# ScalarE's order in a batch of attention: contexts later, one copy of values taken over, one exponential moved up

## The chip, the cores and the metric

The kernel runs on one core of a Trainium2 chip. The metric is device time in microseconds (us) of one execution, all loads from HBM and the stores included. Three runs of the kernel before took 789.79, 789.86 and 788.10 us; their median is 789.79.

## The reference

Two layers work on x of 16 sequences with 128 tokens and 128 features (float32). The change touches only the attention at the head of the first one. For each of the 16 sequences (here: batches):

```python
qkv = (x @ Wqkv.T + bqkv)                       # 16 heads of width 8
attn = softmax(q @ k.T / sqrt(8))               # per head, 128 x 128
coh = sigmoid(tanh([x, cond] @ Wc1.T + bc1) @ Wc2.T + bc2)
mod = attn * coh;  mod = mod / (mod.sum(-1) + 1e-8)
mod = (1 - 0.21) * mod + 0.21 * fa              # fa: one row of weights per batch
x1 = (mod @ v) @ Wout.T + bout
```

After the attention come a product-key expert layer with a batch normalisation over all tokens, a mixture of 8 experts, and a second mixture with hidden width 512. They are unchanged.

## The kernel before

The kernel is written without a scheduler: each engine has its own list of instructions in a fixed order, and semaphores are waited for and raised by hand. An engine that waits holds up everything behind it in its list. Each engine's list for the attention has a function `attend(b, ...)` that is called once per batch b. The stages overlap: while the probabilities of batch b are transposed, the scores of b + 1 are computed and the inputs of b + 2 are projected.

One batch, in the order of the data, with the line that the profile gives:

- PE `project(b)` multiplies the batch's x with four weights into PSUM bank 7 (L461): queries, keys, values, context.
- ScalarE `queries_keys(b)` copies queries (L919) and keys (L921) out of bank 7. ScalarE `values_context(b)` copies the values to v_stage (L925) and takes the tanh of the context (L927); PE's next `project` waits for that tanh (semaphore s_tanh), and so does `coherence(b)`.
- POOL `head_keys(b)` spreads the keys by head, one instruction of 128x512 (L358), when the keys are copied and the scores of b - 1 are through. POOL also stages x (L352) and adds the bias to the values (`values`, L343).
- PE `scores(b)` (L461, 32 rows by 512 columns) waits for L358 and for DVE's last subtraction of the batch before, and fills banks 2 to 5.
- DVE `row_max` (L1205) and `minus_max` (L1212), for the halves q = 0 and 1; ScalarE `exps(b, q)` (L931), an exponential of 128x1024 in place.
- PE `transposes(b, q)` (L501), eight transposes into banks 0 and 1; ScalarE `probs_T(b, q)` (L936) copies both banks to SBUF. Both halves use the same two banks, so the second half's transposes wait for the first half's L936.
- PE `values(b, q)` (L461, 32 small matmuls in all) puts heads' outputs into bank 0 (q = 0) and bank 1 (q = 1). DVE `keep_values(b, q)` (L1219) copies each to oT_heads, and PE `gather(b, q)` brings them to token-major form.
- ScalarE's `ec` (L960) is an exponential of 16 columns from DVE's `tl` (L1281); DVE's cden (L1298), zden (L1302), reciprocal (L1304), o_n (L1306) and o_s (L1312) finish the attention output.
- One batch later: PE `out_T` (L529) transposes it, ScalarE `out_T` (L942) copies it, PE `out_proj` multiplies it with Wout, in the middle of the second half's transposes, and ScalarE `out_x1` (L949) adds the bias.

PE's order in `attend(b)` is: transposes(b, 0), scores(b + 1), out_T(b - 1), transposes(b, 1) with out_proj(b - 1) between its halves, project(b + 2), values(b, 0), values(b, 1), a sum of values, coherence(b + 1), gather(b, 0), gather(b, 1). DVE's order is: tl, row_max(b + 1, 0), minus_max(b + 1, 0), row_max(b + 1, 1), both keep_values(b), minus_max(b + 1, 1), then cden to o_s. In batch 2 DVE also scales the layer's keys (L1252, twice, and L1255), behind minus_max.

ScalarE's order in `attend(b)` before the change is: probs_T(b, 0), out_T(b - 1), out_x1(b - 1), probs_T(b, 1), ec, queries_keys(b + 2), exps(b + 1, 0), exps(b + 1, 1), values_context(b + 2).

Of the kernel before, what the change touches and what calls it, by code (L numbers as in the profile page):

```python
# [22 lines left out]
ACT = mybir.ActivationFunctionType  # L23
# [59 lines left out]
def program(nc, xtok, xT, pA, pL, pC, pR, p8, wq, wqT, down, up, w1, w2, w3, f1, f2, out):  # L83
# [7 lines left out]
    with ExitStack() as ctx:  # L91
# [3 lines left out]
        def sem(name):  # L95
            return ctx.enter_context(nc.semaphore(name))
# [36 lines left out]
        oT_heads = junk[:, 0:512]  # L133
# [23 lines left out]
        def A(name, a=0, b=None):  # L157
            lo, hi = A_AT[name]
            return apack[:, lo + a:hi if b is None else lo + b]
# [5 lines left out]
        def R(name, rows_=P):  # L165
            lo, hi = R_AT[name]
            return rows[0:rows_, lo:hi]
# [54 lines left out]
        def bank(n, a=0, b=512):  # L222
            return banks[:, n, a:b]
# [15 lines left out]

        s_S, s_mx, s_D, s_E, s_T, s_ET, s_pv = (sem("att_" + n) for n in ("S", "mx", "D", "E", "T", "ET", "pv"))  # L240

        s_O, s_sel = sem("att_O"), sem("att_sel")
        s_zd, s_rz, s_on, s_os, s_ostore = sem("s_zd"), sem("s_rzatt"), sem("s_on"), sem("s_os"), sem("s_ostore")

        s_oTp, s_oT, s_x1p, s_x1 = sem("s_oTp"), sem("s_oT"), sem("s_x1p"), sem("s_x1")
# [29 lines left out]
        def wait(eng, s, value):  # L275

            if not isinstance(value, int) or value > 0:
                eng.wait_ge(s, value)

        def col(ap, i):  # L280
            return ap[:, ds(i, 1)] if not isinstance(i, int) else ap[:, i:i + 1]

        def cols(ap, i, n=P):
            return ap[:, ds(i * n, n)] if not isinstance(i, int) else ap[:, i * n:(i + 1) * n]
# [174 lines left out]
        def _(pe):  # L459
            def mm(o, l, r, start=True, stop=True):  # L460
                return pe.matmul(o, l, r, start=start, stop=stop)  # L461
# [33 lines left out]
            def transposes(b, q):  # L495

                pe.wait_ge(s_E, 2 * b + q + 1)
                wait(pe, s_ET, 2 * b + q)
                wait(pe, s_O, 2 * b)
                for g in range(8):  # L500
                    m = pe.transpose(bank(g // FG, P * (g % FG), P * (g % FG) + P), D[q][:, P * g:P * g + P], A("ident"))  # L501
                    if g == 3 and q == 1 and b > 0:
                        out_proj(b - 1)
                m.then_inc(s_T, 1)
# [11 lines left out]

            def gather(b, q):

                pe.wait_ge(s_O, 2 * b + q + 1)
                for j in range(2 * q, 2 * q + 2):  # L520
                    m = mm(bank(6, 9 * FG * j, 9 * FG * j + WIDE), oT_heads[:, P * j:P * j + P], A("sel"))
                if q == 1:
                    m.then_inc(s_sel, 1)
# [7 lines left out]
            def out_proj(b):  # L531
                pe.wait_ge(s_oT, b + 1)
                mm(bank(6, 240, 368), A("woT"), oT).then_inc(s_x1p, 1)
# [377 lines left out]
        def _(act):  # L911
# [3 lines left out]
            def queries_keys(b):  # L915

                act.wait_ge(s_proj, b + 1)
                wait(act, s_S, FG * b)
                act.activation(qT, bank(7, 0, P), ACT.Identity, bias=A("bq"))  # L919
                wait(act, s_kh, b)  # L920
                act.activation(kT, bank(7, P, 2 * P), ACT.Identity, bias=A("bk")).then_inc(s_q, 1)  # L921

            def values_context(b):
                wait(act, s_v, b)
                act.activation(v_stage, bank(7, 2 * P, 3 * P), ACT.Copy).then_inc(s_vst, 1)  # L925
                wait(act, s_coh, b)
                act.activation(thT, bank(7, 3 * P, 4 * P), ACT.Tanh, bias=col(hidb, b)).then_inc(s_tanh, 1)  # L927

            def exps(b, q):
                act.wait_ge(s_D, 2 * b + q + 1)  # L930
                act.activation(D[q], D[q], ACT.Exp, scale=float(HD) ** -0.5).then_inc(s_E, 1)  # L931

            def probs_T(b, q):
                act.wait_ge(s_T, 2 * b + q + 1)
                wait(act, s_pv, 2 * (b - 1) + q + 1)
                act.activation(ET[q], banks[:, 0:2, :].rearrange("p c n -> p (c n)"), ACT.Copy).then_inc(s_ET, 1)  # L936

            def out_T(b):
                act.wait_ge(s_oTp, b + 1)
                wait(act, s_x1p, b)  # L940
                if b < SEEN:
                    m = act.activation(oT, bank(6, 240, 368), ACT.Copy, accum_out=col(o_sum, b))  # L942
                else:
                    m = act.activation(oT, bank(6, 240, 368), ACT.Copy)
                m.then_inc(s_oT, 1)

            def out_x1(b):
                act.wait_ge(s_x1p, b + 1)
                act.activation(cols(x1T_all, b), bank(6, 240, 368), ACT.Identity, bias=A("bout"),  # L949
                               accum_out=col(x1_sum, b)).then_inc(s_x1, 1)  # L950

            def attend(b, more, project_more, first=False):
                probs_T(b, 0)
                if not first:
                    out_T(b - 1)
                    out_x1(b - 1)
                probs_T(b, 1)
                act.wait_ge(s_tl, b + 1)
                wait(act, s_cden, b)
                act.activation(ec, tl, ACT.Exp, scale=-1.0).then_inc(s_ec, 1)  # L960
                if project_more:
                    queries_keys(b + 2)
                if more:
                    exps(b + 1, 0)
                    exps(b + 1, 1)
                if project_more:
                    values_context(b + 2)

            act.wait_ge(dve_setup, DVE_SETUP.index("hid_bias") + 1)
            act.wait_ge(pe_setup, PE_SETUP.index("field2") + 1)  # L970
# [5 lines left out]
                           accum_out=small[0:B, 11:12]).then_inc(act_setup, 1)  # L976
            exps(0, 0)
            exps(0, 1)
            values_context(1)
            attend(0, True, True, first=True)  # L980
            for b in range(1, B - 2):
                attend(b, True, True)
# [183 lines left out]
        def _(v):  # L1166
# [36 lines left out]
            def row_max(b, q):  # L1203
                v.wait_ge(s_S, FG * b + FG)
                v.tensor_reduce(mx4[:, 8 * q:8 * q + 8],  # L1205
                                groups(banks[:, 2 + 2 * q:4 + 2 * q, :].rearrange("p c n -> p (c n)")),
                                AX_X, ALU.max).then_inc(s_mx, 1)
# [5 lines left out]
                                mx4[:, 8 * q:8 * q + 8].unsqueeze(2).broadcast_to([P, 8, P]),  # L1213
                                ALU.subtract).then_inc(s_D, 1)

            def keep_values(b, q):

                v.wait_ge(s_pv, 2 * b + q + 1)
                v.tensor_copy(oT_heads[:, 256 * q:256 * q + 256], bank(q, 0, 256)).then_inc(s_O, 1)  # L1219

            def shifted_scores(b):
                row_max(b, 0)
                minus_max(b, 0)
                row_max(b, 1)
                keep_values(b - 1, 0)
                keep_values(b - 1, 1)
                minus_max(b, 1)

            row_max(0, 0)
# [48 lines left out]
            def attend(b, more):  # L1278
                v.wait_ge(s_coh, b + 1)
                wait(v, s_ec, b)  # L1280
                v.tensor_tensor(tl, bank(6, 368, 368 + NH), R("bc2"), ALU.add).then_inc(s_tl, 1)  # L1281
                if b == B - 2:
                    shift()
                if b == B - 1:
                    centre_last(B - 2)
                    centre(3)
                    keep_values(b, 0)
                    keep_values(b, 1)
                if more:
                    shifted_scores(b + 1)  # L1290
                if b == 2:
                    scaled_keys_of_weights()
                if b == B - 2:
                    for c in range(3):
                        centre(c)

                v.wait_ge(s_ec, b + 1)
                v.tensor_scalar(cden, ec, 1e-8 / (1 - FIELD), (1 + 1e-8) / (1 - FIELD), ALU.mult, ALU.add).then_inc(s_cden, 1)  # L1298
                v.wait_ge(s_sel, b + 1)
                v.wait_ge(s_cden, b + 1)  # L1300
                o9 = bank(6, 0, 144).rearrange("p (h d) -> p h d", d=9)
                v.tensor_tensor(zden.unsqueeze(2), o9[:, :, HD:HD + 1], cden.unsqueeze(2), ALU.mult).then_inc(s_zd, 1)  # L1302
                v.wait_ge(s_zd, b + 1)
                v.reciprocal(rz_att, zden).then_inc(s_rz, 1)  # L1304
                v.wait_ge(s_rz, b + 1)
                v.tensor_tensor(o_n.rearrange("p (h d) -> p h d", d=HD), o9[:, :, 0:HD],  # L1306
                                rz_att.unsqueeze(2).broadcast_to([P, NH, HD]), ALU.mult).then_inc(s_on, 1)
                v.wait_ge(s_on, b + 1)
                v.wait_ge(s_vs, b + 1)
                wait(v, s_oTp, b)  # L1310
                wait(v, s_ostore, min(b, B - 2))
                v.scalar_tensor_tensor(o_s, bank(6, 384, 512), col(fas, b), o_n, ALU.mult, ALU.add).then_inc(s_os, 1)  # L1312
# [432 lines left out]
```

## Time and profile before

| | |
|---|---|
| median of three runs | 789.79 us |
| profiled execution | 790.0 us |
| its span, first to last instruction | 788.2 us |
| PE busy | 740.4 us (94%) |
| DVE busy | 563.2 us (71%) |
| ACT (ScalarE) busy | 569.2 us (72%) |
| POOL busy | 314.9 us (40%) |
| mean granted TensorE clock | 0.989 of full speed |

The first and the last instruction of the profiled execution are 788.2 us apart, and 1.8 us lie around them. The attention takes about the first 150 us of the span. In the rows below, starts are us from the beginning of the span. An instruction that does not depend on the one before it on its engine can start before that one's recorded end. L461, L501 and L529 are PE's; region is one large SBUF tensor in which most tensors of the attention lie, so its name says little; G_both takes the transposed probabilities and W_both the probabilities.

### The profile page before, as it was taken

What the parts mean: (1) busy time and instruction counts of PE and PEld (TensorE: products, weight loads), DVE (VectorE), ACT (ScalarE), POOL (GpSimd) and SP (SyncE); (2) the same over time, 40 slices, a digit from 0 to 9 for tenths busy, and PEclk for the clock granted to TensorE, in tenths of its full rate; (3) what the DMA queues carried; (4) which work ended last, traced back from release to release, by engine and by line L of the source; (5) the groups of instructions that cost most, each with busy time, mean ns of one, the idle gap of its engine ahead of it and who ended that gap; (6) DMA issues with size and microseconds to landing.
All of it is one profiled execution on the core that took longest, in us unless ns stands there. A gap on an engine that the chain in (4) does not pass through costs nothing.

```text
span 788.2 us, 14848 instructions
## 1 busy us (share of the span) xinstructions
PE 740.4 (94%) x5314; PEld 653.7 (83%) x5314; DVE 563.2 (71%) x1511; ACT 569.2 (72%) x985; POOL 314.9 (40%) x230
## 2 busy tenths in 40 slices
PE   4989898979887999999999999999999999999998
PEld 3767676859775799899989989999898899999887
DVE  3788889579379877976986797688679756833422
ACT  2577777359797878978988896898789788553243
POOL 2122231079987175344727442563646071000000
PEclk9999999999997999999999999999999999999999
DMA  8930000000000000000000000000000000000000
GB/s 311 343 108 1 2 2 1 2 1 2 1 1 0 1 1 7 2 1 1 7 2 1 9 0 2 1 8 1 1 2 7 1 1 8 1 1 8 1 1 7
DMA packets 11016, 16.92 MB, mean 21 GB/s; under 512 B 664, under 2 KB 6976, under 8 KB 10688
## 3 DMA queue, kind: packets, MB, share of 16 engines
q1 hardware_dynamic: 10944, 15.98, 6.3%
q8 instruction: 43, 0.70, 0.4%
q14 instruction: 29, 0.24, 0.1%
HBM read 14.93 MB, written 1.05 MB: 20 GB/s over the span
## 4 chain that ended last, share of the span: by engine, by line
PE 84%; DVE 7%; issue 4%; ACT 4%; DMA 1%; SPq 0%; POOL 0%; DVEq 0%; ACTq 0%; POOLq 0%
PE banks L461 78%; PE banks L501 3%; ACT G_both L936 2%; PE banks L698 2%; DVE W_both L1418 1%; DMA region<-in_pR 1%; DVE W_both L1212 1%; ACT region L1006 1%; DVE acc L1563 1%; PE banks L529 1%; DVE HF L1424 0%; ACT region L1012 0%; PE banks L730 0%; DVE pairs L1382 0%; ACT x1T_all L949 0%
## 5 line engine op out<-in xcount | busy, mean ns | idle before, releaser
L403 POOL TENSOR_TENSOR region<-sim 128x1024 f32<-128x1024 f32 x128 | 260.8, 2065 | 99.7 <-DVE top_keys L1375 63.2
L1068 ACT ACTIVATE HF<-banks,lpack 128x256 f32<-128x256 f32 x256 | 105.4, 479 | 55.6 <-PE banks L461 54.6
L1006 ACT ACTIVATE region<-region,neg_thr 128x1024 f32<-128x1024 f32 x128 | 143.8, 1153 | 0.0
L1418 DVE SCALAR_TENSOR_TENSOR W_both<-region,rz_rel,W_both 128x1024 f32<-128x1024 f32 x98 | 137.7, 1405 | 1.7
L461 PE MATMUL banks<-HF,w_sb 128*128 128x256 f32 x512 | 125.0, 388 | 7.8 <-DVE HF L1424 7.7
L461 PEld LDWEIGHTS banks<-f_sb,HF 128*128 128x128 f32 x1024 | 123.7, 192 | 3.4
L1012 ACT ACTIVATE region<-region,dtop 128x1024 f32<-128x1024 f32 x114 | 125.3, 1142 | 0.0
L461 PE MATMUL banks<-f_sb,HF 128*128 128x128 f32 x1024 | 124.5, 275 | 0.0
L461 PE MATMUL banks<-cT,f_sb 128*128 128x256 f32 x512 | 122.7, 382 | 0.1
L461 PEld LDWEIGHTS banks<-HF,w_sb 128*128 128x128 f32 x512 | 95.6, 194 | 20.2 <-DVE HF L1424 8.7
L461 PEld LDWEIGHTS banks<-cT,f_sb 128*128 128x128 f32 x512 | 92.1, 190 | 16.3 <-issue 2.9
L461 PE MATMUL banks<-region 128*128 128x128 f32 (+6 forms) x606 | 90.5, 378 | 8.9 <-DMA region<-in_pC 5.7
L1058 ACT ACTIVATE H<-banks,lpack 128x256 f32<-128x256 f32 x128 | 53.3, 468 | 49.6 <-PE banks L461 49.6
L461 PEld LDWEIGHTS banks<-region 128*128 128x128 f32 (+1 forms) x606 | 67.1, 200 | 19.3 <-issue 11.2
L411 POOL COPY x_all<-x2s 128x128 f32<-128x128 f32 x16 | 11.5, 722 | 163.7 <-DVE x2s L1434 163.7
L1424 DVE TENSOR_SCALAR HF<-banks,lpack 128x256 f32<-128x256 f32 x128 | 55.8, 477 | 23.9 <-PE banks L461 23.6
L461 PEld LDWEIGHTS banks<-w_sb,H 128*128 128x128 f32 x512 | 65.9, 192 | 6.7 <-ACT H L1058 2.8
L461 PE MATMUL banks<-w_sb,H 128*128 128x128 f32 x512 | 68.5, 277 | 2.1 <-DVE acc L1563 1.0
L1563 DVE SCALAR_TENSOR_TENSOR acc_f<-banks,cw,acc_f 128x128 f32<-128x128 f32 x112 | 34.0, 345 | 50.9 <-PE banks L461 50.1
L461 PE MATMUL banks<-x2T,w_sb 128*128 128x256 f32 x256 | 67.1, 385 | 0.0
L461 PEld LDWEIGHTS banks<-x2T,w_sb 128*128 128x128 f32 x256 | 47.6, 193 | 6.3 <-issue 0.5
L931 ACT ACTIVATE W_both<-W_both 128x1024 f32<-128x1024 f32 x32 | 33.9, 1059 | 21.3 <-DVE W_both L1212 21.3
(164 smaller groups left out, 976.1 us busy)
## 6 DMA issues: line engine op xcount, KB each, us to landing
w_sb<-in_w SPq DMA_DIRECT2D x1, 2048.0 KB, 13.0
f_sb<-in_f SPq DMA_DIRECT2D x1, 2048.0 KB, 16.0
region<-in_wq SPq DMA_DIRECT2D x1, 1024.0 KB, 9.0
region<-in_wqT SPq DMA_DIRECT2D x1, 1024.0 KB, 10.8
w_sb<-in_w SPq DMA_DIRECT2D x1, 1024.0 KB, 8.6
out_x<-acc_f SPq DMA_DIRECT2D x16, 64.0 KB, 1.6
region<-in_pA SPq DMA_DIRECT2D x1, 848.5 KB, 4.7
x1T_all<-in_xT SPq DMA_DIRECT2D x1, 768.0 KB, 8.0
```

The source lines that it names most:

```text
L403: pool.tensor_tensor(S[a][h].rearrange("p (i j) -> p i j", i=NK), sim[a][:, h, :].unsqueeze(2).broadcast_to([P, NK, NK]), sim[a][:, PH + h ...
L461: return pe.matmul(o, l, r, start=start, stop=stop)
L501: m = pe.transpose(bank(g // FG, P * (g % FG), P * (g % FG) + P), D[q][:, P * g:P * g + P], A("ident"))
L698: m = pe.transpose(bank(c // 4, P * (c % 4), P * (c % 4) + P), W[a][:, P * c:P * c + P], ident[:, :])
L931: act.activation(D[q], D[q], ACT.Exp, scale=float(HD) ** -0.5).then_inc(s_E, 1)
L1006: act.activation(S[a][h], S[a][h], ACT.Prelu, bias=neg_thr[t % 4][:, h:h + 1], alpha=STEEP).then_inc(h_L, 1)
L1012: act.activation(W[a] if h == 0 and t > 1 else S[a][h], S[a][h], ACT.Exp, bias=dtop[t % 4][:, h, 7:8]).then_inc(h_E, 1)
L1058: m = act.activation(H2[e % 2][:, n, :], bank(H2_BANK[e], 256 * n, 256 * n + 256), ACT.Relu, bias=L("b2", 2 * e + n, 2 * e + n + 1))
L1068: m = act.activation(HF[e % 2][:, f, :], bank(2 + b, 256 * (f % 2), 256 * (f % 2) + 256), ACT.Gelu_apprx_tanh, bias=L("bf", 4 * e + f, 4 * ...
L1418: v.scalar_tensor_tensor(W[a], S[a][h], rz_rel[a][:, h:h + 1], W[a], ALU.mult, ALU.add).then_inc(h_w, 1)
L1424: m = v.tensor_scalar(H1[e % 2][:, n, :], bank(H1_BANK[e], 256 * n, 256 * n + 256), L("b1", 2 * e + n, 2 * e + n + 1), 0.0, ALU.add, ALU.max)
L1563: m = v.scalar_tensor_tensor(dst[:, a, :], y, weight, base, ALU.mult, ALU.add)
```

## The change

ScalarE gets another order for a batch, and one copy goes from DVE to ScalarE:

- probs_T(b, 0), ec, out_T(b - 1), values_context(b + 1), probs_T(b, 1), out_x1(b - 1), keep_values(b) for the first half, exps(b + 1, 0), queries_keys(b + 2), exps(b + 1, 1).
- values_context runs for b + 1 in attend(b), where it ran for b + 2; the call for batch 1 ahead of the loop is gone.
- DVE's keep_values copies the second half alone.
- The semaphore s_O, which counted both copies, becomes s_O0 and s_O1, since two engines now raise them. PE's transposes wait for both and each gather for its own.

```diff
-                wait(pe, s_O, 2 * b)
+                wait(pe, s_O0, b)
+                wait(pe, s_O1, b)
...
-                pe.wait_ge(s_O, 2 * b + q + 1)
+                pe.wait_ge((s_O0, s_O1)[q], b + 1)
...
+            def keep_values(b):
+                act.wait_ge(s_pv, 2 * b + 1)
+                act.activation(oT_heads[:, 0:256], bank(0, 0, 256), ACT.Copy).then_inc(s_O0, 1)
+
             def attend(b, more, project_more, first=False):
                 probs_T(b, 0)
-                if not first:
-                    out_T(b - 1)
-                    out_x1(b - 1)
-                probs_T(b, 1)
                 act.wait_ge(s_tl, b + 1)
                 wait(act, s_cden, b)
                 act.activation(ec, tl, ACT.Exp, scale=-1.0).then_inc(s_ec, 1)
+                if not first:
+                    out_T(b - 1)
+                if more:
+                    values_context(b + 1)
+                probs_T(b, 1)
+                if not first:
+                    out_x1(b - 1)
+                keep_values(b)
+                if more:
+                    exps(b + 1, 0)
                 if project_more:
                     queries_keys(b + 2)
                 if more:
-                    exps(b + 1, 0)
                     exps(b + 1, 1)
-                if project_more:
-                    values_context(b + 2)
...
             exps(0, 0)
             exps(0, 1)
-            values_context(1)
...
-            def keep_values(b, q):
-
-                v.wait_ge(s_pv, 2 * b + q + 1)
-                v.tensor_copy(oT_heads[:, 256 * q:256 * q + 256], bank(q, 0, 256)).then_inc(s_O, 1)
+            def keep_values(b):
+
+                v.wait_ge(s_pv, 2 * b + 2)
+                v.tensor_copy(oT_heads[:, 256:512], bank(1, 0, 256)).then_inc(s_O1, 1)
...
-                keep_values(b - 1, 0)
-                keep_values(b - 1, 1)
+                keep_values(b - 1)
...
-                    keep_values(b, 0)
-                    keep_values(b, 1)
+                    keep_values(b)
```

## Rows read from the trace of the kernel before

**Rows 1.** Busy time by stretch: length, busy us per engine, PE clock, DMA share, GB/s.
```profile
42.31:50.82 8.51, 7.12 (x81) 5.55 (x80) 8.14 (x16) 5.79 (x15) 1.98 (x4) 1.00 0.52 145
50.82:127.98 77.16, 69.81 (x792) 55.34 (x791) 67.83 (x121) 56.75 (x131) 19.79 (x40) 1.00 0.01 2
127.98:135.70 7.72, 6.99 (x81) 5.53 (x79) 7.16 (x15) 5.58 (x13) 1.79 (x3) 1.00 0.00 0
```

**Rows 2.** Chain of waits within one batch: start, length, what.
```profile
94.04 1.07 PE banks L461 x8
...
95.37 0.42 issue
```

**Rows 3.** Timeline of ScalarE in one batch: start, length, engine, line, operation.
```profile
89.40 1.02 ACT L936 ACTIVATE G_both<-banks 128x1024 f32<-128x1024 f32 x1
...
90.43 0.36 ACT L919 ACTIVATE region<-banks,region 128x128 f32<-128x128 f32 x1
90.68 0.37 ACT L921 ACTIVATE region<-banks,region 128x128 f32<-128x128 f32 x1
...
93.30 1.06 ACT L931 ACTIVATE W_both<-W_both 128x1024 f32<-128x1024 f32 x1 [1.31 <-DVE W_both L1212]
94.26 0.26 ACT L925 ACTIVATE region<-banks 128x128 f32<-128x128 f32 x1
...
94.67 1.02 ACT L936 ACTIVATE G_both<-banks 128x1024 f32<-128x1024 f32 x1
```

**Rows 4.** Timeline of DVE in the same batch.
```profile
91.27 0.86 DVE L1219 COPY region<-banks 128x256 f32<-128x256 f32 x2
...
93.18 0.17 DVE L1298 TENSOR_SCALAR region<-region 128x16 f32<-128x16 f32 x1
...
94.54 0.17 DVE L1281 TENSOR_TENSOR region<-banks,region 128x16 f32<-128x16 f32 x1
```

**Rows 5.** Two copies of 128x256 from PSUM by source line (ns min/median/max).
```profile
L1219 DVE COPY region<-banks x32: 424/424/425, 28.7 to 148.0; 128x256 f32<-128x256 f32 x32
...
L1042 ACT ACTIVATE cT<-banks x8: 366/383/386, 268.0 to 754.4; 128x256 f32<-128x256 f32 x8
```

**Rows 6.** Timeline of DVE and PE in the step into batch 3.
```profile
46.09 1.28 DVE L1252 TENSOR_TENSOR region<-region 128x512 f32<-128x512 f32 x2
...
48.78 0.17 DVE L1281 TENSOR_TENSOR region<-banks,region 128x16 f32<-128x16 f32 x1
...
49.10 0.30 PE L529 MATMUL banks<-region 128*128 128x128 f32 x1 [1.08 <-DVE region L1281]
```

**Rows 7.** Timeline of POOL and PE in the batch of rows 3.
```profile
91.12 1.04 POOL L358 TENSOR_TENSOR region<-region 128x512 f32<-128x512 f32 x1 [3.86 <-ACT region L921]
...
93.97 1.14 PE L461 MATMUL banks<-region 32*128 32x512 f32 x8
95.04 0.33 PE L529 MATMUL banks<-region 128*128 128x128 f32 x1
```

**Rows 8.** Timeline of POOL and PE at batch 0.
```profile
10.72 1.04 POOL L358 TENSOR_TENSOR region<-region 128x512 f32<-128x512 f32 x1 [3.61 <-ACT region L921]
...
11.90 1.24 PE L461 MATMUL banks<-region 32*128 32x512 f32 x4 [2.08 <-POOL region L358]
```

**Rows 9.** Timelines of DVE and POOL in the expert stages, where they meet.
```profile
209.63 2.39 POOL L403 TENSOR_TENSOR region<-sim 128x1024 f32<-128x1024 f32 x1
...
211.97 0.21 DVE L1400 TENSOR_TENSOR dtop<-top 128x64 f32<-128x64 f32 x1
211.98 1.96 POOL L403 TENSOR_TENSOR region<-sim 128x1024 f32<-128x1024 f32 x1
...
230.79 1.09 DVE L1488 COPY picked<-best 128x4 f32<-128x4 f32 x1
...
241.68 3.00 DVE L1418 SCALAR_TENSOR_TENSOR W_both<-region,rz_rel,W_both 128x1024 f32<-128x1024 f32 x1
241.69 1.91 POOL L403 TENSOR_TENSOR region<-sim 128x1024 f32<-128x1024 f32 x1
```

More of the change, by code:

```diff
@@ L240, in program @@
         s_S, s_mx, s_D, s_E, s_T, s_ET, s_pv = (sem("att_" + n) for n in ("S", "mx", "D", "E", "T", "ET", "pv"))
-        s_O, s_sel = sem("att_O"), sem("att_sel")
+        s_O0, s_O1, s_sel = sem("att_O0"), sem("att_O1"), sem("att_sel")
         s_zd, s_rz, s_on, s_os, s_ostore = sem("s_zd"), sem("s_rzatt"), sem("s_on"), sem("s_os"), sem("s_ostore")
```

## The prediction

> **What bounds the kernel now.** I read the page first, then busy time by stretches, then the chain of waits in one batch, then the timeline of that batch for each engine. PE's share is near full on the page's busy line, but it is an average over stages, and the change touches the attention stage alone. So the question is what paces that stage. The windows [rows 1] are cut at the starts of ScalarE's second copy of transposed probabilities (L936, probs_T(b,1)); I call such a start E. A batch takes 7.72 us. Thirteen of the steps from E of batch 0 (26.88) to E of batch 14 (135.70) do: the one at 127.98, two like it, and ten in 50.82:127.98 (77.16 us). The step from batch 2 to 3 takes 8.51, since DVE has three extra instructions there (L1252 twice, L1255). The step behind 135.70 is of another form: DVE's centring and the out_T behind it set its end. In a regular batch no engine is full: of 7.72 us PE is busy 6.99, DVE 7.16 and ACT 5.58 in that window.
>
> The chain [rows 2] stays on PE from the values through gather, transposes, scores and out_T, and then stands 0.42 us at 95.37. ScalarE's timeline [rows 3] says why: the next transposes need the banks that L936 empties, and L936 started at 94.67 although the first transposes were over by 94.04, where the chain goes on with the scores. It was behind the value copy and tanh (L925, L927: from 94.26 to 94.67, 0.41 us), and these behind the exponential at 93.30, which waited for DVE. So today's loop is values, two copies on DVE, subtraction, exponential, value copy and tanh, L936, transposes, L936, values.
>
> All places below are us after E = 89.40.
>
> **What the change takes away.** Value copy and tanh leave the stretch between exponential and L936 for the idle time after out_T: 0.41 us a batch off that loop. Their new place has room: out_T's copy starts there at 6.4 and the next E is at 7.8, and ScalarE's old x1 copy in that hole has moved behind E. The first copy of values leaves DVE, but this shortens nothing on the loop: the pair took 0.86 us where one takes 0.424 [rows 4, 5], so the second did not overlap the first and was waiting for its own matmuls. It stays at 91.27 + 0.86 - 0.42 = 91.71, or 2.31. At most it would start 0.09 us earlier (the overlap that 90.43 and 90.68 show between two ScalarE instructions of 0.36), and the exponential that it feeds is not on the new path. By this loop alone the step would be 7.72 - 0.41 = 7.31. PE has a floor of its own: without the 0.42 us stand, out_T would still end at 5.97 (95.37), and from there to E there is a fixed piece. Batch 3 shows that piece bare [rows 6]: out_T ends at 49.10 + 0.30 = 49.40, E follows at 50.82, that is 1.42 us (copy, out_proj, second half of the transposes). 5.97 + 1.42 = 7.39: the most that the change could give is 0.33 us a batch.
>
> **What it puts in the way.** Scores of the next batch but one need the keys' per-head product on POOL (L358), and this needs queries_keys, which now stands behind three things. Step by step:
> - The first copy of values on ScalarE starts when PE has delivered: DVE's started at 91.27, and DVE was waiting, so 1.87. I take the same for ScalarE; it could be 0.02 earlier or later.
> - A 128x256 copy from PSUM takes 0.383 on ScalarE [rows 5]. What follows starts 0.10 before an instruction's end there (93.30 + 1.06 against 94.26, 90.43 + 0.36 against 90.68) [rows 3], so after 0.28: exps(b+1,0) starts at 2.15.
> - Exponential to next instruction: 93.30 to 94.26, 0.96. Queries at 3.11.
> - queries to keys 0.25 (90.43 to 90.68): keys at 3.36. Keys to L358 0.44 (90.68 to 91.12) [rows 7]: L358 at 3.80. It takes 1.04: end 4.84.
> - From its end to PE: batch 0 has it bare [rows 8], 10.72 + 1.04 = 11.76, scores at 11.90, so 0.14. Scores at 4.98.
> Now they start at 93.97, or 4.57 [rows 7], in line behind the transposes. From their start to out_T's end 95.04 + 0.33 - 93.97 = 1.40; then the piece of 1.42. E to E becomes 4.98 + 1.40 + 1.42 = 7.80, against 7.72: plus 0.08 us, 13 times, 1.1 us. The cover that queries_keys loses is thus just larger than the gain: L358 used to end at 2.76, with 1.8 us to spare.
>
> The moved ec (L960, tiny) and x1 do not bind: x1 is wanted by a matmul behind the values, and T0 (first transposes, 3.60) wants the exponential that ends at 2.15 + 1.06 = 3.21. The two semaphores add a wait that is already met. In the step into batch 3 out_T is late for DVE's sake (49.10) and remains so. The last step and the tail are set by DVE's centring and by PE; the table load moves behind the copy of values but is still over before out_T of batch 15. I cost these at nothing; were the cover of the table load gone, it would cost at most 1 us once.
>
> **A collision.** Moving L358 from 1.72 to 3.80 puts it on DVE's cden (L1298, 93.18, or 3.78) [rows 4]. Small DVE instructions can stand still while POOL works: a copy of 4 columns took 1.09 us at 230.79 [rows 9]. The Trainium skill, "SBUF — State Buffer", section "Who interferes with whom", says that tensor_scalar and copy in a two-port mode, and DVE instructions with two SBUF inputs, need a port pair that GpSimd holds for its whole instruction, whoever starts first. This trace agrees with the blocking (the 1.09). By that page alone L358 would have to wait for cden's 0.17, and the step would be 7.97.
> Near ties [rows 9]: the 128x64 subtraction at 211.97 was 0.01 us ahead of POOL; it took 0.21, too short for a wait, and POOL took 1.96. But the weighted sum at 241.68, ahead by as little, took 3.00 beside a POOL instruction of 1.91: it waited that one out. cden is small and 0.02 ahead, so I take the first: L358 is 0.05 to 0.06 longer, the step 7.86, plus 0.14. Bounds: nothing (7.80), and cden held to L358's end. In that case cden ends at about 4.86 instead of 3.95, tl starts 0.91 later than 94.54 (5.14 now), at 6.05; out_T follows tl by 0.32 (48.78 to 49.10) [rows 6], at 6.37, and E by 1.72 (49.10 to 50.82), at 8.09: plus 0.37.
> In batch 2 the two 128x512 products of L1252 (1.28 us together) [rows 6] start where cden else does. The nearest row is a POOL instruction that met such a DVE sum of 128x512 just ahead of it: 2.39 for 1.91, 0.48 [rows 9]. L358 would end at 5.3, the second product would wait for it, from 4.4 to about 5.3, and all behind it to E too: plus 0.9, once. Between 0 and 1.1.
>
> **Sum.** 13 x 0.14 = 1.8 and 0.9: plus 2.7 us. The profiled execution took 790.0 (span 788.2), the median is 789.79; 789.8 + 2.7 = 792.5. All after attention hangs on it in series and on loads that are in by 50 us, so the sum passes through.
>
> **Rivals.**
> 1. *The collision costs nothing*, cden being out of L358's way: 13 x 0.08 = 1.1, 790.9. For it: cden reads 16 columns, and 0.05 us decides. The legs of the sum are good to 0.07 a batch together, so this case reaches from 789.9 to 791.9. Chance 0.30.
> 2. *POOL wins*: L358 takes the port first and cden waits each time: 13 x 0.37 + 0.9 = 5.7, 795.5. For it: the row at 241.68; 0.02 us is less than what I know of the copy's start. Against it: the row at 211.97. Chance 0.20.
> 3. *Faster*: the 0.42 us stand goes and nothing takes its place. It needs scores at 4.57 or earlier, so the key chain shorter by 0.41 than its legs above; then 7.39, 13 x 0.33 = 4.3 less, 785.5. It decides at E to scores: every 0.1 below 4.90 is 1.3 us gained against now. Only a copy on ScalarE that starts well before DVE's could do it, and it can't before PE has finished. Chance 0.08.
> The forecast (792.5, own range 791.2 to 794.0) has 0.40; 0.02 is left.
>
> **How the numbers follow.** No change means within 0.3%, 2.4 us, about what a measurement here can tell. The forecast lies mostly above that line: slower 0.28, same 0.12. Rival 1 is same (0.28) and slower (0.02), rival 2 slower (0.20), rival 3 faster (0.08). With the rest: slower 0.51, same 0.40, faster 0.09. Range 789.9 to 795.9: below it rival 3 and the edge of rival 1, above it little of rival 2.
>
> **What the profile after would show.** L936 to L936 of 7.8 to 7.9 us; the PE stand of 0.42 gone from behind out_T and one of 0.3 to 0.4 between first transposes and scores, released by L358; L358 at 3.8 after E, long 1.04 (rival 1) or 1.1; cden 0.17 long, or about 1.0 (rival 2); out_proj released by ScalarE's out_T copy. In batch 2 L1252 longer than 1.28 for two. I am wrong if scores start right behind the transposes (rival 3), if the copy on ScalarE doesn't start near 1.87, or if L358 is no longer what PE waits for.

## The result, and the profile after

The changed kernel takes 792.3 us (median of 18 runs), the kernel before beside it 789.62 (18 runs): ratio 1.0032, 95% interval 1.0021 to 1.0043, so 2.5 us slower (1.7 to 3.4). The forecast was 792.5. The profiled execution of the changed kernel took 793.8 (span 792.0).

Busy time by stretch, changed kernel, cut at E (columns as in [rows 1], which these rows answer):

```profile
34.62:42.39 7.77, 7.13 (x81) 5.57 (x80) 6.37 (x12) 6.09 (x15) 1.93 (x4) 1.00 1.05 353
42.39:51.77 9.38, 7.19 (x81) 5.59 (x80) 8.88 (x15) 6.19 (x14) 2.97 (x4) 1.00 0.49 134
51.77:129.42 77.65, 71.28 (x792) 55.64 (x791) 63.26 (x111) 60.83 (x141) 19.38 (x40) 1.00 0.01 2
137.09:145.96 8.87, 6.16 (x73) 5.34 (x72) 7.29 (x15) 5.16 (x10) 0.46 (x1) 1.00 0.01 2
145.96:792.00 646.04, 623.56 (x4075) 562.40 (x4073) 448.27 (x1298) 478.42 (x783) 282.18 (x157) 0.98 0.01 3
```

A regular step is 7.76 to 7.77 us (77.65 for ten; the first is 7.81, the last 7.67) where it was 7.72, and the step into batch 3 is 9.38 where it was 8.51. The last step is shorter, 8.87 against 9.60: before's trace has PE at half clock (1.2 GHz) for 3.4 us of it, from 143.3; e3, whose regular steps are those of before, takes 8.87 there at full clock. E of batch 15 comes 0.66 us later than before (145.96 against 145.30); without that half-clock time it would be 1.4. The last row has the rest of the kernel, in which nothing was changed: 646.04 against 642.90.

Timeline of one batch of the changed kernel, all engines, E = 82.83. It answers to [rows 3, 4, 7]; L937 was L936, L932 was L931, L955 is ScalarE's new copy, L920 and L922 are queries and keys, L1303 is cden, L530 is out_T:

```profile
82.83 1.02 ACT L937 ACTIVATE G_both<-banks 128x1024 f32<-128x1024 f32 x1 [0.59 <-PE banks L502]
...
84.70 0.38 ACT L955 ACTIVATE region<-banks 128x256 f32<-128x256 f32 x1 [0.50 <-PE banks L461]
84.98 1.05 ACT L932 ACTIVATE W_both<-W_both 128x1024 f32<-128x1024 f32 x1
...
85.92 0.36 ACT L920 ACTIVATE region<-banks,region 128x128 f32<-128x128 f32 x1
86.17 0.37 ACT L922 ACTIVATE region<-banks,region 128x128 f32<-128x128 f32 x1
...
86.61 0.17 DVE L1303 TENSOR_SCALAR region<-region 128x16 f32<-128x16 f32 x1
86.62 1.05 POOL L358 TENSOR_TENSOR region<-region 128x512 f32<-128x512 f32 x1 [5.83 <-ACT region L922]
86.72 1.06 ACT L932 ACTIVATE W_both<-W_both 128x1024 f32<-128x1024 f32 x1 [0.18 <-DVE W_both L1219]
...
87.69 1.01 ACT L937 ACTIVATE G_both<-banks 128x1024 f32<-128x1024 f32 x1
87.77 1.14 PE L461 MATMUL banks<-region 32*128 32x512 f32 x8 [0.31 <-issue]
...
88.84 0.33 PE L530 MATMUL banks<-region 128*128 128x128 f32 x1
...
90.59 1.02 ACT L937 ACTIVATE G_both<-banks 128x1024 f32<-128x1024 f32 x1 [0.59 <-PE banks L502]
```

Read it as distances from E: copy 1.87, exponential 2.15, queries 3.09, keys 3.34, head product 3.79, scores 4.94, out_T 6.01, next E 7.76. The chain of the changed kernel shows PE's stand where it was forecast, ahead of the scores, and none behind out_T, where [rows 2] had 0.42:

```profile
86.59 0.87 PE banks L502 x8
87.47 0.31 issue
87.77 1.14 PE banks L461 x8
88.91 0.26 PE banks L530
89.17 0.44 PE banks L502 x4
```

The step into batch 3, DVE and POOL (answers to [rows 6]; L1258 are the two key products):

```profile
46.17 2.13 DVE L1258 TENSOR_TENSOR region<-region 128x512 f32<-128x512 f32 x2
46.18 1.57 POOL L358 TENSOR_TENSOR region<-region 128x512 f32<-128x512 f32 x1 [5.83 <-ACT region L922]
...
47.70 0.75 POOL L352 COPY region<-x1T_all 128x128 f32<-128x128 f32 x1
...
50.05 0.30 PE L530 MATMUL banks<-region 128*128 128x128 f32 x1 [1.06 <-DVE region L1287]
```

The two products take 2.13 us instead of 1.28, the head product 1.57 instead of 1.04, and the small copy behind it 0.75 instead of 0.29: each waits for the other side. PE stands 0.82 us ahead of the scores, where before it stood nowhere, and 1.06 ahead of out_T, as before (1.08). It is DVE's delay that sets this step: tl (L1287, at 49.74) comes 7.35 after E where it came 6.47 (48.78), and out_T waits for it; the later scores are through by then.

### The profile page after: what moved, and what is told of

The parts are those of the page before. It is cut to its first block, busy times and chain, and to the rows that moved or that the text cites. A ratio compares the mean times of both kernels' runs of the same rounds, so it can differ in the third digit from the quotient of the medians.

```text
span 792.0 us, 14878 instructions
## 1 busy us (share of the span) xinstructions
PE 745.3 (94%) x5314; PEld 656.4 (83%) x5314; DVE 556.9 (70%) x1495; ACT 575.6 (73%) x1001; POOL 315.3 (40%) x230
## 3 DMA queue, kind: packets, MB, share of 16 engines
HBM read 14.93 MB, written 1.05 MB: 20 GB/s over the span
## 4 chain that ended last, share of the span: by engine, by line
PE 87%; DVE 5%; ACT 4%; issue 3%; DMA 1%; POOL 0%; DVEq 0%; SPq 0%; ACTq 0%; POOLq 0%
PE banks L461 80%; PE banks L502 4%; ACT G_both L937 2%; PE banks L699 2%; DVE W_both L1423 1%; ACT region L1019 1%; DVE W_both L1219 1%; ACT region L1013 1%; DMA region<-in_pC 1%; PE banks L530 1%; DVE acc L1568 0%; PE banks L731 0%; DVE pairs L1387 0%; DVE PT L1520 0%; PE banks L790 0%
## 5 line engine op out<-in xcount | busy, mean ns | idle before, releaser
L461 PE MATMUL banks<-x2T,w_sb 128*128 128x256 f32 x256 | 69.0, 394 | 0.0
L358 POOL TENSOR_TENSOR region<-region 128x512 f32<-128x512 f32 x16 | 17.3, 1082 | 95.8 <-ACT region L922 95.8
```

What stands on the lines that cost most here:

```text
L358: pool.tensor_tensor(k_heads.rearrange("p (g n) -> p g n", g=FG), kT.unsqueeze(1).broadcast_to([P, FG, P]), A("head4").unsqueeze(2).broadc ...
```

## Experiments

My theory: the change frees 0.4 us a batch behind the exponential and loses it, and more, to the chain queries_keys, head product, scores; the copy on ScalarE gains nothing; key scaling and head product collide once. Rivals: the copy on ScalarE is what costs, or DVE's share is what binds, or the rest of the kernel pays. Ratios are against runs of the kernel before on the same chip (788.6 us in the first group, 789.3 in the second, 788.9 in the third).

**e1: keys ahead of the copy.**

```diff
+                if project_more:
+                    queries_keys(b + 2)
                 keep_values(b)
                 if more:
                     exps(b + 1, 0)
-                if project_more:
-                    queries_keys(b + 2)
-                if more:
                     exps(b + 1, 1)
```

> The changed kernel, with queries_keys ahead of ScalarE's copy of the first values and of exps(b+1,0). Places are us after E, the start of ScalarE's second L936-type copy of a batch. Theory (the key chain queries_keys, POOL's head product, scores paces the changed kernel): the head product starts at about 2.0 instead of 3.8, scores start right behind the first transposes at 4.57, and a step from E to E takes 7.39 to 7.43 us instead of 7.76 in the changed kernel and 7.72 before. The collision with DVE's key scaling in batch 2 goes too: that step takes 8.5, not 9.38. Sum against before: 13 x -0.31 = -4.0 us, about 785.5 us. Rival (the copy on ScalarE is what costs): the step stays at 7.7 or more and the time is not below that of before.

784.18 us, ratio 0.9948 (0.9935 to 0.9960): 4 us faster than before. In its timeline (here of the one step that takes 7.54) the head product starts 1.97 after E and scores 4.57:

```profile
93.61 1.02 ACT L937 ACTIVATE G_both<-banks 128x1024 f32<-128x1024 f32 x1 [0.59 <-PE banks L502]
...
95.58 1.04 POOL L358 TENSOR_TENSOR region<-region 128x512 f32<-128x512 f32 x1 [3.78 <-ACT region L922]
...
98.18 1.14 PE L461 MATMUL banks<-region 32*128 32x512 f32 x8
```

Twelve steps are 7.30 to 7.43 us, one is 7.54 (in it out_T came late, at 99.43), and the step into batch 3 is 8.50. With one call moved, the change's loss of 2.5 us is a gain of 4: the key chain is the cause. (This takes in the step into batch 3, 0.88 of it.)

**e2: contexts later, all copies of values left on DVE, keys first.** The kernel before, with `attend` in this order. ec and out_x1 stand in their new places too, and the call for batch 1 ahead of the loop is gone:

```diff
                 probs_T(b, 0)
-                if not first:
-                    out_T(b - 1)
-                    out_x1(b - 1)
-                probs_T(b, 1)
...
                 act.activation(ec, tl, ACT.Exp, scale=-1.0).then_inc(s_ec, 1)
+                if not first:
+                    out_T(b - 1)
+                if more:
+                    values_context(b + 1)
+                probs_T(b, 1)
+                if not first:
+                    out_x1(b - 1)
...
-                if project_more:
-                    values_context(b + 2)
```

> The kernel before, with only the contexts a batch later (and x1 behind the second transposed copy, ec early); queries_keys ahead of the exponentials; DVE keeps both copies of values. Theory: the whole gain comes from this part. DVE's second row maximum now ends at about 2.1 after E, so its two copies of values start some 0.1 to 0.2 later than with one on ScalarE; step 7.43 to 7.50, key scaling step 8.5, sum -2.9 to -3.8 us, about 786 to 787 us. Rival (moving a copy off DVE is what a shorter step needs): step stays near 7.7, no change from before.

785.66 us, ratio 0.9956 (0.9944 to 0.9969), regular step 7.39 (7.43 to 7.50 expected). DVE's two copies did start late (96.03, 2.00 after E) but took 0.74 together instead of 0.86, so its subtraction started at 2.66 as ever (96.69; before 92.05, 2.65):

```profile
96.03 0.74 DVE L1219 COPY region<-banks 128x256 f32<-128x256 f32 x2
96.69 1.21 DVE L1212 TENSOR_TENSOR W_both<-banks,region 128x1024 f32<-128x1024 f32 x1
...
97.93 1.06 ACT L931 ACTIVATE W_both<-W_both 128x1024 f32<-128x1024 f32 x1 [1.07 <-DVE W_both L1212]
98.90 1.01 ACT L936 ACTIVATE G_both<-banks 128x1024 f32<-128x1024 f32 x1
```

So the gain needs no copy on ScalarE, and it is the contexts': L936 follows the exponential by 0.97 us (97.93 to 98.90) where it was 1.37 (93.30 to 94.67), and PE's stand of 0.42 is gone from the chain. ec and out_x1, moved with them, show no part in it. out_x1 had stood ahead of E, but E follows the end of the transposes by 0.04 before and by 0.03 in e2, and the exponential waits for DVE's subtraction in both.

**e3: the copy on ScalarE, nothing else.** The kernel before, with DVE's, PE's and the semaphores' part of the change, and on ScalarE:

```diff
                 if project_more:
                     queries_keys(b + 2)
+                keep_values(b)
                 if more:
                     exps(b + 1, 0)
```

> The kernel before, with only the first copy of values on ScalarE, between queries_keys and exps(b+1,0); contexts stay at the end. Theory: DVE's second copy already waited for its own matmuls, so the loop through DVE's subtraction, exponential, contexts and transposed copies is as long as before: step 7.72, sum 0 (within 0.5 us). Rival (DVE's share is the bound): each batch 0.34 shorter, -4.4 us. Rival (the copy on ScalarE costs): longer steps.

788.97 us, ratio 1.0006 (0.9997 to 1.0015); regular step 7.71 to 7.72. Neither DVE's share nor the copy's cost on ScalarE sets the step.

**e4: the changed kernel, contexts back at the end.**

```diff
                 if not first:
                     out_T(b - 1)
-                if more:
-                    values_context(b + 1)
                 probs_T(b, 1)
...
                 if more:
                     exps(b + 1, 1)
+                if project_more:
+                    values_context(b + 2)
```

> The changed kernel with values_context back at the end of a batch, so only the move of the contexts is undone. Theory: with the key chain binding, the contexts' new place is worth nothing: step 7.76 to 7.80, key scaling step 9.4, the time within 0.5 us of the changed kernel's 792.3, about 2.5 us above before. Rival (the contexts' move does gain 0.41 in the changed kernel and something else costs more): step about 8.1 to 8.2, about 797 us.

797.85 us, ratio 1.0110 (1.0094 to 1.0125), step 8.41. My expectation (7.76 to 7.80, about 792) was wrong by 6 us. The rival's time, about 797, was met, but its step of 8.1 to 8.2 was not. The timeline names what I had left out:

```profile
93.29 0.45 POOL L343 TENSOR_TENSOR region<-region 128x128 f32<-128x128 f32 x1
...
93.77 0.28 ACT L926 ACTIVATE region<-banks 128x128 f32<-128x128 f32 x1 [0.57 <-POOL region L343]
93.95 0.36 ACT L928 ACTIVATE region<-banks,region 128x128 f32<-128x128 f32 x1
94.20 1.03 ACT L937 ACTIVATE G_both<-banks 128x1024 f32<-128x1024 f32 x1
```

The value copy overwrites v_stage, so it waits for POOL's `values`, and in POOL's list this stands behind the head product and the staging of x. With a late head product it is late too, and in its old place the value copy would carry that to L937. So the contexts' move is worth 0.64 us a step in the changed kernel (8.41 to 7.77), not nothing: it hid a second way from the late keys to the end of the batch.

**e5: the changed kernel again**, unedited.

> The changed kernel once more, beside others on the same chip. In its profile the steps from E to E sum to only 1.4 us over before without the stretch at half clock that before's profile shows at 143.3; the remaining excess of its profile (about 3 us) lies behind 205 us, where it shows a stretch of 10.2 us at half clock against 6.8 us before. Theory (that was one execution's clock): the timed runs stay 2 to 3.5 us over before, but this profile's part behind the last E is within 1.5 us of the 642.8 us of before, and 13 steps of 7.76 and one of 9.38 come back to 0.02. Rival (the shift itself brings the longer stretch): the part behind the last E is again about 646.

791.5 us beside 789.3, ratio 1.0038 (1.0026 to 1.0051). Its part behind the last E is 790.8 - 147.8 = 643.0 us, as before the change, not 646. The other half of the expectation missed: the steps did not all come back. In this execution PE had 3.4 us of half clock at 50.6, behind its wait of the step into batch 3 (the row below, columns as in [rows 1]), and that step and the next took 10.12 and 8.19:

```profile
50.60:54.00 3.40, 3.40 (x17) 3.14 (x15) 2.76 (x3) 1.93 (x7) 0.00 (x0) 0.51 0.00 0
```

```profile
42.35 1.02 ACT L937 ACTIVATE G_both<-banks 128x1024 f32<-128x1024 f32 x1 [0.59 <-PE banks L502]
...
52.47 1.02 ACT L937 ACTIVATE G_both<-banks 128x1024 f32<-128x1024 f32 x1 [1.31 <-PE banks L502]
...
60.66 1.02 ACT L937 ACTIVATE G_both<-banks 128x1024 f32<-128x1024 f32 x1 [0.59 <-PE banks L502]
```

**e6: keys between copy and exponential.** The changed kernel, with:

```diff
                 keep_values(b)
+                if project_more:
+                    queries_keys(b + 2)
                 if more:
                     exps(b + 1, 0)
-                if project_more:
-                    queries_keys(b + 2)
-                if more:
                     exps(b + 1, 1)
```

> The changed kernel with queries_keys between ScalarE's copy of values and exps(b+1,0). POOL's head product then starts at 2.84 after E and ends at 3.88, so it is under way when DVE's cden comes at 3.78. Theory: exps(b+1,0) ends at 3.70, 0.2 late for the first transposes; scores start at about 4.77 and a step takes 7.55 to 7.65 us; cden is stretched from 0.17 to 0.25 to 0.35 us, the product keeps 1.04 (whoever starts first holds the port), and this costs nothing since DVE has 0.5 us to spare there. Sum -1 to -2.5 us against before. Rival (a held port costs the engine that holds it too): the product is longer than 1.04 in regular batches.

788.9 us beside 789.3, ratio 0.9994 (0.9984 to 1.0005); regular step 7.61, as expected, the sum less clear of zero than I said. cden took 0.17, not 0.25 to 0.35, though it started at 3.78 and the product's recorded end was 3.89:

```profile
83.47 1.04 POOL L358 TENSOR_TENSOR region<-region 128x512 f32<-128x512 f32 x1 [4.88 <-ACT region L922]
84.40 0.17 DVE L1302 TENSOR_SCALAR region<-region 128x16 f32<-128x16 f32 x1
```

This was no test of the port. A DVE instruction that was held ends only 0.03 us behind the recorded end of POOL's (e9, below); this one ends 0.06 behind it, so a wait here would not show. The time of the head product (1.97, 2.85, 3.79 after E) goes with the step (7.39, 7.61, 7.77) over three kernels; in e6 it is the exponential, late for the transposes, that carries it.

**e7: e1 with out_proj behind the second transposes; e8: the same on e2.**

```diff
                 for g in range(8):
                     m = pe.transpose(...)
-                    if g == 3 and q == 1 and b > 0:
-                        out_proj(b - 1)
                 m.then_inc(s_T, 1)
+                if q == 1 and b > 0:
+                    out_proj(b - 1)
```

> Keys first (as in e1), and PE's out_proj moved from the middle of the second transposes to behind them. Theory: in e1 the step of 7.39 is PE's chain up to out_T (5.97) and then ScalarE's out_T copy, out_proj and half the transposes (1.42). With out_proj behind, the second transposes wait only for the emptied banks (5.98) and take 1.05: step 7.08 to 7.18, about 4 us below e1, 780 us. Rival (PE's order is not what paces it, or DVE takes over at once): step 7.3 or more.

> The kernel before with contexts later and out_proj behind the second transposes; DVE keeps both copies of values. Theory: here DVE's two copies follow its second row maximum late, at 9.4 us minus the step, so the step settles where 7.08 plus that delay meets it, about 7.25: 0.1 to 0.15 above e7, some 782 us. That is what the copy on ScalarE is worth once nothing else binds. Rival (DVE's copy never matters): the same step and time as e7.

e7: 782.14 us, ratio 0.9911 (0.9897 to 0.9925), regular step 7.06 to 7.08. e8: 782.09, ratio 0.9917 (0.9903 to 0.9930), step mostly 7.23. The steps came out as worked out (7.08 to 7.18 and about 7.25), so the copy on ScalarE is worth 0.16 us a batch once contexts, keys and out_proj are out of the way. e7's time did not: 780 was expected. In the timed medians the two are equal, so that 2 us is not seen there. In the two profiled executions the rest of the kernel gives it back: behind the last E e7 takes 645.61 and e8 642.48, over the same instructions. e7 has some 17 us at half clock there, e8 some 14; the rest of the 3 us is unexplained.

**e9: the changed kernel, key scaling moved.**

```diff
+                if b == 3:
+                    scaled_keys_of_weights()
                 if more:
                     shifted_scores(b + 1)
-                if b == 2:
-                    scaled_keys_of_weights()
```

> The changed kernel, with DVE's key scaling of batch 2 (two 128x512 products and a small one) moved from behind its second subtraction to the place behind tl in batch 3, where DVE waits 0.9 us for scores and POOL has nothing. Theory (the 9.38 step is DVE and POOL wanting one SBUF port, and the same work elsewhere is nearly free): the two products take 1.28 us again instead of 2.13, POOL's head product 1.04 to 1.06 instead of 1.57; the steps around batch 3 take 7.76 and at most 8.3 instead of 9.38; 1 to 1.6 us below the changed kernel, about 790.3 beside 791.5 to 792.3. If PE's long wait there is also what brings a half-clock stretch near 50 us, up to 1 us more. Rival (the extra 0.87 is simply a later product chain, no port): the two products still take about 2.1.

789.05 us beside 788.91, ratio 1.0001 (0.9989 to 1.0013); steps 7.76 and 8.10 in place of 9.38 and 7.77. The head product takes 1.05 again. The two products do not take the 1.28 that I expected but 1.52, and POOL's last copy 0.76, since they met there:

```profile
46.77 1.52 DVE L1258 TENSOR_TENSOR region<-region 128x512 f32<-128x512 f32 x2
...
46.99 0.76 POOL L348 COPY region<-region 128x128 f32<-128x128 f32 x1
```

The step of 8.10 holds what rival 2 asked for. DVE is late there, its cden comes 0.21 us behind the head product instead of just ahead of it, and waits until that is through:

```profile
53.11 1.04 POOL L358 TENSOR_TENSOR region<-region 128x512 f32<-128x512 f32 x1 [5.37 <-ACT region L922]
53.32 0.86 DVE L1303 TENSOR_SCALAR region<-region 128x16 f32<-128x16 f32 x1
...
55.38 0.16 DVE L1287 TENSOR_TENSOR region<-banks,region 128x16 f32<-128x16 f32 x1
...
55.69 0.30 PE L530 MATMUL banks<-region 128*128 128x128 f32 x1 [0.29 <-DVE region L1287]
```

From E (49.31) tl comes at 6.07, out_T at 6.38, the next E at 8.10; the prediction had 6.05, 6.37 and 8.09 for this case.

The edit takes back all that the change had lost against before, 2.5 us of which the traced steps explain 1.3. The other 1.2 is within what the two intervals allow together (0.9 to 1.0 us either way each).

**e10: e7 with the key scaling moved.**

> The kernel of e7 (contexts later, keys first, out_proj behind the second transposes, one copy on ScalarE) with the same move of the key scaling. DVE has only 0.2 to 0.5 us to spare in e7, so some of the 1.4 us shows: the step of 8.12 becomes 7.07 and the next 7.9 to 8.2. Expected 0 to -0.5 us against e7, 781.5 to 782.2. Rival (it lands on DVE's path in full): 0.3 us above e7.

780.45 us beside 788.91, ratio 0.9892 (0.9877 to 0.9907), the best of the series. The steps came as expected, 7.08 and 7.85. The time came 1 us below the range, and the intervals of e7 and e10 overlap; from the first E to the last, e10 takes 108.60 and e7 108.70, so the steps do not explain the difference. Its chain has PE in every piece but one of 0.09 us:

```profile
68.39 1.06 PE banks L502 x8
69.45 1.12 PE banks L461 x10
70.57 0.09 issue
70.66 2.60 PE banks L461 x44
73.26 0.88 PE banks L502 x8
```

## Why the prediction was right, and where its sum was not

- *What bounds.* Right: the 0.42 us stand went, and one of 0.31 came ahead of the scores.
- *The second copy gains nothing on DVE.* Right: it starts at 85.13, 2.30 after E (2.31 forecast), and e3 shows 7.72.
- *The key chain.* Each leg came within 0.04 us: 1.87, 2.15, 3.09, 3.34, 3.79 against 1.87, 2.15, 3.11, 3.36, 3.80. From the product's end (87.67) to scores it was 0.10, not 0.14; batch 0, where I read it [rows 8], ran before PE was busy. Scores to next E took 2.82, as said. e1 shows the cause.
- *The near tie with cden.* cden was 0.01 ahead and was not held, the row I chose. But L358 took 1.05, 0.01 more and not 0.05 to 0.06. The Trainium skill's rule ("SBUF — State Buffer", "Who interferes with whom": whichever of the two starts first keeps the pair) would have had it wait out cden; this trace shows no such wait for an instruction of 16 columns, twelve times over. Step 7.77 against 7.86, half of it from here and half from the 0.10 above: this term was mis-sized, 0.05 x 13 = 0.6 us instead of 1.8. The order was close to turning: with POOL ahead, once in e9, cden took 0.86 and the step 8.10. That was rival 2, and its price (8.09) was right.
- *Key scaling.* Forecast plus 0.9, measured 9.38 - 8.51 = 0.87, and both engines were held as said. Here the trace agrees with that rule, for both sides: 2.13 for 1.28 and 1.57 for 1.04. e9 shows it.
- *The sum.* 0.6 + 0.87 = 1.5 us are in the steps, where I had 2.7; by the last E it is 1.4, since E of batch 0 came 0.07 earlier. The timed runs say 2.5 (1.7 to 3.4). So the total was met partly by luck. What remains, about 1 us, stays open. PE's clock is one candidate: the timed runs of the changed kernel had a mean granted clock of 0.984 (23 runs), those of before in the three groups 0.987 (45 runs), and within the first 18 runs of the changed kernel those at 0.980 have a median of 792.4, those at 0.989 one of 791.2. e5 shows one such loss, 0.74 + 0.42 us around 50 us, and the first profile another behind the attention, 10.2 us of half clock from 214.6. Against it: among before's 45 runs the clock does not order the times (788.6 at 0.985, 789.5 at 0.989). That the long PE wait of the step into batch 3 brings the clock down is not shown: three traces have the waits of 0.82 and 1.06 us (the first profile, e4, e5), and only e5 has half clock behind them.
- *What I left out.* POOL's list behind the head product (e4). It did not show in the changed kernel since the contexts had been moved, and I had not seen that they needed to be.
- *Rivals.* Nothing of rival 2 in the changed kernel (cden never waits there; once in e9). Rival 1 is nearest to the steps (0.05 against 0.08 a batch), though not in batch 2. Rival 3's condition, scores at 4.57, is e1, and gives its 7.39.

## What to carry to other kernels

A call that moves to a later place in one engine's list moves all that it releases: follow its product through the other engines' lists up to the next user, and compare with what the user had to spare (here 1.8 us of cover, all spent). When two edits are made together, work out each alone: here one was worth 3.5 us, one nothing, and the order between them lost that and 2.5 more. Before moving an SBUF-to-SBUF instruction of POOL, look what DVE reads from SBUF at its new place, and the other way round.

## What the runs showed of the hardware

- A DVE product of two SBUF tensors and a POOL product, started 0.01 us apart, each held the other up: together 0.85 us longer on DVE, 0.53 on POOL. A DVE instruction of 16 columns, also 0.01 ahead, cost POOL 0.01 and nothing itself, twelve times each in the traces of the changed kernel, e4, e5 and e9. The same instruction 0.21 us behind POOL's start took 0.86 instead of 0.17 and ended 0.03 behind POOL's recorded end (e9).
- ScalarE started on the values 1.87 us after E, as DVE had (91.27).
- PE ran at half clock for stretches of 3.4 to 10.2 us that moved from run to run; 3.4 us of it cost 0.73 us in the last step of before, and 1.16 over two steps of e5.
